# Attention: the moments of the residual sum by running sums on ScalarE, and TensorE's step in the order router, turn, products

## What is computed

```python
h = layernorm(x)
w = softmax((h @ w_lin.T) per head over its 31 taps)
a[t] = sum over k of w[t, k] * h[t - 30 + k]      # per head
x2 = x + layernorm(a)                             # the residual sum
yn = layernorm(x2)                                # input of the experts
logits = yn @ gate_w.T                            # 16 experts, and the shared gate
out = x2 + layernorm(experts(yn) + shared(yn))
```

## Time and profile before

| | before |
|---|---|
| median of 3 runs | 1089.03 us (1088.56 to 1089.05) |
| the profiled execution's own time | 1088.95 us |
| its span | 1086.9 us |
| busy: PE, PEld, DVE | 959.6, 843.6, 861.3 us (88%, 78%, 79%) |
| busy: ACT, POOL | 557.3, 489.6 us (51%, 45%) |
| granted clock of TensorE, mean | 0.95 of full speed |

### The profile page before, as it was taken

The page is one execution under the profiler, slowest core; times in us unless marked ns, Lnnn a source line. Parts: engine busy times, 40 slices in busy tenths (PEclk is TensorE's granted clock), DMA queues, the critical chain, the costliest instruction groups (busy, mean ns, idle before and its releaser), DMA issues. The chain is left out here.

```text
span 1086.9 us, 27047 instructions
## 1 busy us (share of the span) xinstructions
PE 959.6 (88%) x9256; PEld 843.6 (78%) x9257; DVE 861.3 (79%) x2402; ACT 557.3 (51%) x1314; POOL 489.6 (45%) x715
## 2 busy tenths in 40 slices
PE   5998898998899768887897999999998799999995
PEld 4767787886788657766676998999987688888884
DVE  5977998797999668888885688788884578878777
ACT  5994445899144532333235455555553345554553
POOL 4452556421355400000002665566644786777762
PEclk9998999999899769899989899999999899999998
DMA  5532678633468630221123655555575465555541
GB/s 170 170 96 70 185 228 253 197 123 84 116 191 241 204 117 15 79 72 49 49 68 107 153 172 170 165 168 171 171 156 174 150 180 175 175 169 189 157 145 49
DMA packets 154723, 156.86 MB, mean 144 GB/s; under 512 B 52480, under 2 KB 134528, under 8 KB 154624
## 3 DMA queue, kind: packets, MB, share of 16 engines
q1 hardware_dynamic: 136048, 112.40, 33.5%
q0 software_dynamic: 13056, 35.67, 12.3%
q10 hardware_dynamic: 5520, 7.47, 2.3%
HBM read 91.38 MB, written 64.11 MB: 143 GB/s over the span
## 5 line engine op out<-in xcount | busy, mean ns | idle before, releaser
L806 POOL DMA_INDIRECT xg<-yn_scratch,ids x144 | 136.9, 951 | 282.9 <-DVE ids L1046 188.0
L1334 POOL DMA_INDIRECT cy<-expert_rows,slots x128 | 146.1, 1141 | 54.1 <-issue 35.8
L765 PE MATMUL bank<-yh,gh 128*128 128x512 f32 x352 | 144.8, 411 | 19.4 <-DVE s_hf L745 9.1
L647 PE MATMUL bank<-xbd,am 128*32 128x68 f32 x4096 | 138.2, 304 | 11.0 <-DMA xbd<-xn_scratch 6.6
L765 PE MATMUL bank<-yl,gh 128*128 128x512 f32 x352 | 142.3, 404 | 0.0
L765 PE MATMUL bank<-yh,gl 128*128 128x512 f32 x352 | 141.9, 403 | 0.0
L647 PEld LDWEIGHTS bank<-xbd,am 128*32 128x32 f32 x4096 | 122.8, 129 | 18.5 <-issue 8.8
L765 PEld LDWEIGHTS bank<-yh,gh 128*128 128x128 f32 x352 | 68.8, 195 | 33.8 <-DVE s_hf L745 7.9
L1208 PE MATMUL bank<-eh,xh 128*128 x288 | 94.0, 327 | 0.6 <-DVE xl L1252 0.6
L1252 DVE TENSOR_TENSOR xl<-bank,xh 128x256 fp32r<-128x256 f32 x144 | 61.1, 424 | 34.1 <-ACT xh L1234 27.0
L1234 ACT ACTIVATE xh<-bank 128x256 fp32r<-128x256 f32 x144 | 55.2, 384 | 61.5 <-PE bank L1184 61.0
(11 more groups left out here) (191 smaller groups left out, 2865.7 us busy)
## 6 DMA issues: line engine op xcount, KB each, us to landing
expert_rows<-yo SPq DMA_DIRECT2D x144, 128.0 KB, 1.8
xbd<-xn_scratch SPq DMA_DIRECT2D x128, 72.0 KB, 2.3
xt<-xp SPq DMA_DIRECT2D x32, 256.0 KB, 2.7
xn_scratch<-xn SPq DMA_DIRECT2D x64, 128.0 KB, 2.7
xr<-x SPq DMA_DIRECT2D x32, 256.0 KB, 3.6
x_scratch<-x SPq DMA_DIRECT2D x32, 256.0 KB, 3.5
yn_scratch<-yn SPq DMA_DIRECT2D x32, 256.0 KB, 3.7
ynt_scratch<-ynt SPq DMA_DIRECT2D x32, 256.0 KB, 4.4
```

Source lines behind the costliest of these rows:

```text
L647: ins = nc.tensor.matmul(pso[q][t][J * b:J * b + J, g * MW:(g + 1) * MW], am[:, q, g, e, side], xbd[:, q, e + side, :, g], start=(g == 0 a ...
L765: ins = self.nc.tensor.matmul(self.pb[2 * k + half][:], w[:, c, col:col + P], y[:, n % 2, c, :], start=(j == 0), stop=(j == 5))
L806: return nc.gpsimd.indirect_dma_start(out=to, out_offset=None, in_=yn_d.rearrange("n p c -> (n p) c"), in_offset=bass.IndirectOffsetOnAxis ...
L1334: nc.gpsimd.indirect_dma_start(out=y[:, r, t, j], out_offset=None, in_=yg_d, in_offset=bass.IndirectOffsetOnAxis(ap=slots[:, 2 * unit + t, ...
```

## The change

`moments3` moves from VectorE to ScalarE and is done in two passes there. The first is a copy of a tile of `x2` times -1/256 with a running sum over the row: the sum is minus the mean and goes into `shift2`. The second is the square of the tile with that as bias and a running sum: 256 times the variance, into `mv2`. What the passes write besides goes to `unused`. It stands in ScalarE's step between `put_logits` and `centred`, for unit i - 3 (on VectorE it was for unit i - 2). GpSimd's scales divide the sum by the count with one instruction more; the shift of `x2` comes from ScalarE, and so that of `av` alone is negated. `divided` gets a wait for the residual of two units before.

TensorE's step gets the order `router`, `turn_yn`, both halves of `products`. For units 0 to 9 and 16 to 31 the logits go to banks 4 and 5 in turn instead of `psy`, and the turn no longer waits for their copy; for units 10 to 15, beside which the taps of the second half use those banks, they stay in `psy` with the wait.

```diff
@@ -192,7 +192,8 @@
         rstd2 = sb("rstd2", [P, 2, 4])
         shift2 = sb("shift2", [P, 2, 4])
         x2 = sb("x2", [P, 2, 2, C])
-        st3 = sb("st3", [P, 2, 2, 6])
+        unused = sb("unused", [P, 4, C], BF16)
+        by_count = sb("by_count", [P, 2])
         yn = sb("yn", [P, 2, 2, C])
         ynt = sb("ynt", [P, 2, 2, CC, P])
         gws = sb("gws", [P, CC, GW])
@@ -207,13 +208,22 @@
             psx_full xth_ok xtl_ok psl_full mx_ok sub_ok exp_ok pse_full probs_ok
             xs_in0 xs_in1 am_ok pso_full rs_ok av_ok st2_ok mv2_ok var2_ok dev2_ok norm2_ok
             z_ok xr_in0 xr_in1 x2_ok st3_ok mv3_ok yn_ok psy_full ynt_ok psg_full lg_ok
-            x2_out0 x2_out1 yn_out0 yn_out1 ynt_out0 ynt_out1 g_in g_hi""".split()
+            x2_out0 x2_out1 yn_out0 yn_out1 ynt_out0 ynt_out1 mean_ok shift_ok shift2_ok g_in g_hi""".split()
         s = {n: sem(n) for n in names}
         block = ctx.enter_context(nc.Block())
         psx, psl, pse = (pb[0][:, 0:C], pb[0][:, C:2 * C]), (pb[2:4], pb[4:6]), (pb[1], pb[6])
         pso, psy = (pb[0:2], pb[2:4]), (pb[7][:, 0:C], pb[7][:, C:2 * C])
         xn_rows = xn_d.rearrange("a b j c -> (a b) j c")
         PLACES = 2 + 4 * HS
+        ROUTED = 6
+
+        def apart(n):
+            return n >= NCH or n + ROUTED < NCH
+
+        def logits_place(n, t):
+            if apart(n):
+                return pb[4 + n % 2][:, t * C:t * C + GW]
+            return psy[t][:, 0:GW]
 
         def flow(taps_step, product_step):
             for i in range(-4, NPR):
@@ -306,9 +316,10 @@
             nc.gpsimd.memset(zero[:], 0.0).then_inc(s["zeros"], 1)
             nc.gpsimd.memset(neg_half[:], -0.5).then_inc(s["consts"], 1)
             nc.gpsimd.memset(eps[:], EPS).then_inc(s["consts"], 1)
+            nc.gpsimd.memset(by_count[:], 1.0 / C).then_inc(s["consts"], 1)
             nc.gpsimd.memset(ident[:], 0.0).then_inc(s["consts"], 1)
             po.wait_ge(s["zeros"], 1)
-            po.wait_ge(s["consts"], 3)
+            po.wait_ge(s["consts"], 4)
             nc.gpsimd.affine_select(out=ident[:], in_=ident[:], compare_op=ALU.not_equal, fill=1.0, base=0,
                                     pattern=[[-1, P]], channel_multiplier=1).then_inc(s["ident_ok"], 1)
 
@@ -321,7 +332,7 @@
                     nc.gpsimd.memset(ones[:], 1.0).then_inc(s["consts"], 1)
                     nc.gpsimd.memset(mask[:], 1.0).then_inc(s["consts"], 1)
                     nc.gpsimd.iota(top.iota[:], pattern=[[-1, E]], base=E, channel_multiplier=0).then_inc(s["consts"], 1)
-                    po.wait_ge(s["consts"], 6)
+                    po.wait_ge(s["consts"], 7)
                     po.wait_ge(s["places_ok"], 2)
                 if 3 <= i < 3 + HS:
                     k = i - 3
@@ -339,11 +350,18 @@
 
             def scales(n, q, mv_, rstd_, shift_, k, lo, hi):
                 w = hi - lo
+                if hi == 4:
+                    nc.gpsimd.tensor_tensor(mv_[:, q, 2:4, 1], mv_[:, q, 2:4, 1], by_count[:], ALU.mult).then_inc(s["mean_ok"], 1)
+                if lo == 0:
+                    nc.gpsimd.tensor_tensor(shift_[:, q, 0:2], zero[:, 0:2], mv_[:, q, 0:2, 0], ALU.subtract).then_inc(s[f"shift{k}_ok"], 1)
+                if hi == 4:
+                    po.wait_ge(s["mean_ok"], n // (NCH + 2) * NCH + n % (NCH + 2) - 1)
                 nc.gpsimd.tensor_tensor(rstd_[:, q, lo:hi], mv_[:, q, lo:hi, 1], eps[:, 0:w], ALU.add).then_inc(s[f"var{k}_ok"], 1)
-                nc.gpsimd.tensor_tensor(shift_[:, q, lo:hi], zero[:, 0:w], mv_[:, q, lo:hi, 0], ALU.subtract).then_inc(s[f"var{k}_ok"], 1)
-                po.wait_ge(s[f"var{k}_ok"], n * 2 + 2)
+                po.wait_ge(s[f"var{k}_ok"], n + 1)
                 nc.gpsimd.tensor_tensor(rstd_[:, q, lo:hi], rstd_[:, q, lo:hi], neg_half[:, 0:w], ALU.pow).then_inc(s[f"dev{k}_ok"], 1)
                 po.wait_ge(s[f"dev{k}_ok"], n + 1)
+                if lo == 0:
+                    po.wait_ge(s[f"shift{k}_ok"], n + 1 if k == "" else n // (NCH + 2) * NCH + n % (NCH + 2) + 1)
                 nc.gpsimd.tensor_tensor(shift_[:, q, lo:hi], shift_[:, q, lo:hi], rstd_[:, q, lo:hi], ALU.mult).then_inc(s[f"norm{k}_ok"], 1)
 
             def scales1(n):
@@ -444,6 +462,7 @@
                     m = n * 2 + t
                     pv = pso[q][t][:, 0:NG * MW].rearrange("p (g w) -> p g w", g=NG)
                     ve.wait_ge(s["pso_full"], n + 3)
+                    ve.wait_ge(s["x2_ok"], n * 2 + 2)
                     nc.vector.reciprocal(rs[:, t].rearrange("p (k g) -> p g k", g=NG),
                                          pv[:, :, SLOT_C:MW]).then_inc(s["rs_ok"], 1)
                     ve.wait_ge(s["rs_ok"], m + 1)
@@ -461,15 +480,6 @@
                     wait_apart(ve, s["ve_passed"], s["st2_ok"], m + 1)
                     nc.vector.bn_aggr(mv2[:, q, t], st2[:, q, t]).then_inc(s["mv2_ok"], 1)
 
-            def moments3(n):
-                ve.wait_ge(s["norm2_ok"], n // NCH * (NCH + 2) + n % NCH + 1)
-                for t in range(2):
-                    ve.wait_ge(s["x2_ok"], n * 2 + t + 5)
-                    nc.vector.bn_stats(st3[:, n % 2, t], x2[:, n % 2, t]).then_inc(s["st3_ok"], 1)
-                for t in range(2):
-                    wait_apart(ve, s["ve_passed"], s["st3_ok"], n * 2 + t + 1)
-                    nc.vector.bn_aggr(mv2[:, n % 2, 2 + t], st3[:, n % 2, t]).then_inc(s["mv3_ok"], 1)
-
             def taps_step(h, i):
                 at(h, i - 1, spread)
                 at(h, i + 1, low)
@@ -482,7 +492,6 @@
             def product_step(h, i):
                 at(h, i + 1, masked)
                 at(h, i - 1, divided)
-                at(h, i - 2, moments3)
             flow(taps_step, product_step)
             top.done(ve, nc.vector.tensor_copy(top.rev[:], top.iota[:]))
             ve.wait_ge(s["lg_ok"], top.EARLY + 2)
@@ -534,7 +543,20 @@
                 for t in range(2):
                     m = n * 2 + t
                     act.wait_ge(s["psg_full"], n * 2 + 2)
-                    nc.scalar.activation(logits[:, m:m + 1, :], psy[t][:, None, 0:GW], ACT.Copy).then_inc(s["lg_ok"], 1)
+                    nc.scalar.activation(logits[:, m:m + 1, :], logits_place(n, t)[:, None, :], ACT.Copy).then_inc(s["lg_ok"], 1)
+
+            def moments3(n):
+                q = n % 2
+                if n > 0:
+                    act.wait_ge(s["mv3_ok"], n * 2)
+                for t in range(2):
+                    act.wait_ge(s["x2_ok"], n * 2 + t + 5)
+                    nc.scalar.activation(unused[:, t], x2[:, q, t], ACT.Copy, scale=-1.0 / C,
+                                         accum_out=shift2[:, q, 2 + t:3 + t]).then_inc(s["st3_ok"], 1)
+                for t in range(2):
+                    act.wait_ge(s["st3_ok"], n * 2 + t + 1)
+                    nc.scalar.activation(unused[:, 2 + t], x2[:, q, t], ACT.Square, bias=shift2[:, q, 2 + t:3 + t],
+                                         accum_out=mv2[:, q, 2 + t, 1:2]).then_inc(s["mv3_ok"], 1)
 
             def centred(n):
                 q = n % 2
@@ -585,7 +607,8 @@
                                          ).then_inc(s["g_hi"], 1)
 
             def product_step(h, i):
-                at(h, i - 6, put_logits)
+                at(h, i - ROUTED, put_logits)
+                at(h, i - 3, moments3)
                 at(h, i - 2, centred)
                 at(h, i - 4, normal2)
                 at(h, i - 5, turned)
@@ -655,7 +678,10 @@
                 for t in range(2):
                     m = n * 2 + t
                     pe.wait_ge(s["yn_ok"], m + 5)
-                    pe.wait_ge(s["lg_ok"], n * 2 + 2)
+                    if n > 0:
+                        pe.wait_ge(s["ynt_ok"], n * 2)
+                    if n == 0 or not apart(n - 1):
+                        pe.wait_ge(s["lg_ok"], n * 2 + 2)
                     for c in range(CC):
                         ins = nc.tensor.transpose(psy[t][:, c * P:(c + 1) * P], yn[:, n % 2, t, c * P:(c + 1) * P], ident[:])
                     ins.then_inc(s["psy_full"], 1)
@@ -664,9 +690,11 @@
                 if n == 0:
                     pe.wait_ge(s["gw_in"], 16)
                 pe.wait_ge(s["ynt_ok"], n * 2 + 2)
+                if n > 1:
+                    pe.wait_ge(s["lg_ok"], n * 2)
                 for t in range(2):
                     for c in range(CC):
-                        ins = nc.tensor.matmul(psy[t][:, 0:GW], ynt[:, n % 2, t, c], gws[:, c, :],
+                        ins = nc.tensor.matmul(logits_place(n, t), ynt[:, n % 2, t, c], gws[:, c, :],
                                                start=(c == 0), stop=(c == CC - 1))
                     ins.then_inc(s["psg_full"], 1)
 
@@ -676,9 +704,9 @@
                 at(h, i, taps)
 
             def product_step(h, i):
-                at(h, i - 6, router)
+                at(h, i - ROUTED, router)
+                at(h, i - 5, turn_yn)
                 at(h, i, lambda n: products(n, 0))
```

(1 more changed line is left out.)

## The result

The changed kernel takes 1110.03 us (median of 4 runs, 1108.77 to 1114.01) against 1089.04 us for the kernel before on the same chip: a ratio of 1.0198, with a 95% interval of 1.0175 to 1.0221. It is 21 us slower; 1112.9 was forecast.

A forecast was written before the change was run, and what follows sets the result against it. A GpSimd-ScalarE ring was taken to bound the attention step, with TensorE's step as long. Longer steps (+21.6 us) and the ends (+2.3) sum to +23.9 on 1088.95: 1112.9 us, range 1100 to 1121.

The forecast's parts named there:

- The ring GpSimd to ScalarE and back: Attention step: residual, scales on GpSimd, `centred`, `normal2` on ScalarE, then the next residual; 5.78 us, no slack.
- TensorE's order: Router, then turn, then products: TensorE's own step falls from 5.83 to 5.6 us, worth 0 in a 6.9 us step.
- VectorE's moments: VectorE loses 1.16 us a step of moments of `x2`; alone worth nothing, it only makes VectorE early.
- What the meeting costs: Masked products run beside GpSimd's residual and scales; step grows to 6.9 us, +21.6 us over twenty steps.
- ScalarE's four passes: Four added ACTIVATEs between the logits and `centred` cost 1.9 us a step, hidden in a step of 6.9.
- the cycle of 6.0 us: ScalarE's own work per attention step, 4.1 + 1.9 us including the four new ACTIVATEs; bounds 5.4 to 7.0.
- GpSimd's wait for ScalarE's sums, SP, the logits' copy: 0: Attention steps: GpSimd's scales waiting for ScalarE's sums, SP's loads, and units 11 to 15's logits wait each cost 0.
- VectorE's new wait in `divided`: 0: VectorE waits for the residual of two units before, said to be done a step ago; costs 0.
- The ends: End of the attention's second half: ScalarE's longer cycle and unit 15's longer chain add 2.3 us (0 to +6).
- The faster one: Rival: masked products start 2 us or more after the residual and miss GpSimd; 1085.6 us, chance 0.16.
- The cancelling case: Rival: few GpSimd instructions caught, a short read-out, a step of 5.8 us; 1089 us, chance 0.10.
- the one with ScalarE as the bound: Rival: no hindrance, four ACTIVATEs at 2.4 us make ScalarE's cycle 6.5 us; 1107 us, chance 0.10.

The follow-up runs named there:

- experiment 1: Kernel before the change, with only TensorE's new order and the logits' own banks, moments left on VectorE: ratio 1.0008 to the kernel before.
- experiment 2: Changed kernel with ScalarE's four passes over the residual sum left out, two tiny copies in their place: 1106.39 us, ratio 1.0182 to the kernel before.
- experiment 3: Changed kernel with the mask copied into PSUM, so masked products read one tile from SBUF: 1088.13 us, ratio 1.0006 to the kernel before.
- 8: Changed kernel with three buffers of `x2` in place of two, mask still in SBUF: ratio 1.0025 to the kernel before.
- experiment 7: Kernel before the change, with the mask in PSUM and nothing else: ratio 0.9990 to the kernel before.
- experiment 5: Changed kernel with the mask in PSUM and ScalarE's passes ahead of the copy of the logits: ratio 0.9978 to the kernel before.
- experiment 6: Kernel before the change, with TensorE's new order, the logits' own banks and the mask in PSUM: ratio 0.9977 to the kernel before.
- experiment 4: Changed kernel with VectorE's step turned round, `divided` ahead of the masked products: 1095.99 us, ratio 1.0075 to the kernel before.

## Why the prediction was right, point by point

- **What bounds the kernel.** The ring GpSimd to ScalarE and back: right. TensorE's order alone (experiment 1) does not move the step of the kernel before, and leaving out ScalarE's work (experiment 2) does not move that of the changed one; freeing the ring (experiments 3 and 8) does. TensorE's old order is a second limit of the same length (experiment 7), which the prediction had in its 5.83 us.
- **VectorE's moments are worth nothing in themselves.** No run takes them away alone, but where nothing meets they are worth nothing that can be told: 0.9978 with them moved (experiment 5), 0.9977 with them on VectorE (experiment 6). That they held the masked products back is shown by what they do after the change: they start with the residual in the step shown, 0.13 us before it.
- **What the meeting costs.** Right in kind, a little long in size: 6.9 us a step forecast, 6.80 and 6.84 measured, +19.9 us for +21.6. The residual pays more than in the earlier trace rows (2.27 us for two, against 2.11), the scales less: one of them on the whole, not two.
- **ScalarE's four passes.** Hidden in the steady step, as said. Their price of 1.9 us was 1.78; the cycle of 6.0 us was 5.7. The trace now shows what a sum costs: a separate read-out of 188 to 196 ns follows each pass. The passes by themselves take 420 and 495 ns. By the formula of the Trainium skill (ScalarE: Activation LUTs, What ACT_TABLE_LOAD costs), which has no read-out, the estimate is 399 and 492 ns.
- **GpSimd's wait for ScalarE's sums, SP, the logits' copy: 0.** Nothing in the step of the timeline waits for them: L354 follows the residual at once.
- **VectorE's new wait in `divided`: 0.** Right for the time, wrong in its reason. The sum that it asks for was not done a step ago: it is the residual that has just run. VectorE waits for it 0.71 us once in the stretch (at 140.53), which costs nothing as VectorE is ahead. In experiment 4 it waits 1.38 us there at 143.02, and this is part of why its masked products come so late.
- **TensorE's order: 0 in such a step.** Right by experiment 1, and so is its price where TensorE is the limit: 5.82 against 5.6 us. But the end of the second half has no such cover, and there the order is worth 1.2 us, which the prediction left out: from unit 12 to the table load experiment 1 takes 30.77 us, the kernel before 31.97.
- **The ends.** +2.3 forecast, 3.1 measured (31.97 to 35.09 us from unit 12 to the table load), and that these are so close is in part luck. The passes, which were the forecast, make 2.1 (experiment 2). Two things that it did not have cancel in part: the 1.2 us that TensorE's order gives back, and a second meeting of the same kind, to which the difference leaves some 2.2. VectorE, early here too, begins its search for the two best experts while GpSimd still has the last residual and its scales. The end of the second half in the changed kernel:

```profile
393.82 2.31 POOL L386 TENSOR_TENSOR x<-av,xr 128x256 f32<-128x256 f32 x2 [3.27 <-ACT yn L574]
...
395.58 1.50 DVE L138 SCALAR_TENSOR_TENSOR ew<-ew,logits 128x896 f32<-128x896 f32 x1
...
396.10 1.04 POOL L354 TENSOR_TENSOR mv<-mv,by_count 128x2 f32<-128x2 f32 x1
...
398.27 1.11 POOL L365 TENSOR_TENSOR shift<-shift,rstd 128x2 f32<-128x2 f32 x1
...
399.41 1.09 ACT L574 ACTIVATE yn<-x,shift,rstd 128x256 f32<-128x256 f32 x2 [1.27 <-POOL shift L365]
```

The last two sums take 2.31 us, and three small instructions around 1 us each (L354, L365, and L359 at 399.61) where one takes 0.20, beside instructions of VectorE's search that also read two tiles from SBUF (L138, and L133 and L134 after it). ScalarE waits 1.27 us for the last shift. No run takes this meeting away alone.
- **The rivals.** The faster one needed the masked products to miss GpSimd; experiment 3 is that case by other means, and it gives 1088, since ScalarE's cycle of 5.7 us comes next, and experiment 5, with that moved too, 0.22% less than before, near the 1085.6 us of the rival. VectorE was as full as the prediction said, and taking work from it made the kernel slower. The cancelling case and the one with ScalarE as the bound fall too: the step is 6.8 us, and without ScalarE's passes it stays so.

## What to carry to other kernels

An engine that is busy all the time need not be the limit: look for a ring of hand-overs through engines that are half idle, and compare its length with the step. Two limits of one length hide each other: easing one alone gains nothing. Work that is taken from a full engine makes its other instructions earlier; look what they then run beside, above all VectorE instructions with two operands in SBUF beside GpSimd. Where such a meeting can't be avoided in time, move one operand to PSUM, or give the ring another buffer.

## What the runs showed that was not expected

- Where GpSimd and VectorE meet, both pay: the masked products are 934 ns for 677, and four of them can take 3.57 us for 2.46.
- In the changed kernel TensorE idles before the router in each step (7.9 us in the 45 us stretch), and the records give a granted clock of 0.84 there, between the two levels of 1.2 and 2.4 GHz, against 1.00 before. But the 128 products take as long at the lower figure: 4.20 us from 139.89, in a stretch at 0.58, and 4.21 us from 132.51, in one at 1.00. So the lower figure in this stretch is not a slower TensorE while it works. At the end of the attention it is: from 394 to 411 us the granted clock is 0.50, the level of 1.2 GHz, TensorE idles 0.8 to 4.1 us before each router, and the router takes 1.89 us for 1.07.
